# Output norm's deviation by ScalarE's root and a VectorE refinement in place of GpSimd's power, and three more blocks of spike additions on GpSimd

## What is computed

```python
def lif(x, v_th): return (x - v_th >= 0)            # a "spike", 0 or 1
def layer_norm(x, g, b):
    return (x - mean(x)) * rsqrt(var(x) + 1e-5) * g + b

# attention, 16 heads of 16
Q, K, V = (lif(layer_norm(xn @ W.T + bias, g, beta), 1.0) for each of q, k, v)
attn = 16 - (q_sum + k_sum.T - 2 * Q @ K.T) + log_pe_bias      # no softmax
out  = lif((attn * scale) @ V, 0.5)
out  = lif(layer_norm(out @ Wo.T + bo, go, betao), 1.0)

# experts: top 2 of softmax(xn @ router.T), scores made to sum to 1
h = xn @ up[e];  y = (silu(h[:256]) * h[256:]) @ down[e]
ffn = sum over the two experts of score * y

result = x + out + ffn
```

## Time and profile before

| | |
|---|---|
| median of 3 runs | 449.91 us (449.11 to 450.32) |
| the profiled execution, its own time | 448.21 us |
| its span in the profile | 446.3 us |
| mean granted clock of TensorE, share of full | 0.939 |
| TensorE busy | 389.5 us (87%) |
| VectorE busy | 283.8 us (64%) |
| ScalarE busy | 237.0 us (53%) |
| GpSimd busy | 210.7 us (47%) |

### The profile page before, as it was taken

The page is one execution under the profiler, slowest core; times in us unless marked ns, Lnnn a source line. Parts: engine busy times, 40 slices in busy tenths (PEclk is TensorE's granted clock), DMA queues, the critical chain, the costliest instruction groups (busy, mean ns, idle before and its releaser), DMA issues.

```text
span 446.3 us, 8933 instructions
## 1 busy us (share of the span) xinstructions
PE 389.5 (87%) x2585; PEld 318.6 (71%) x2586; DVE 283.8 (64%) x717; ACT 237.0 (53%) x756; POOL 210.7 (47%) x211
## 2 busy tenths in 40 slices
PE   4479956767999998899999999999999998999871
PEld 1223655767999997788888888888888875777550
DVE  5887899994777787644444444444444433479996
ACT  1436835342888888445445454454454543466650
POOL 3215330003677200177777777734333332369984
PEclk9596979686999999999999999999999999999976
DMA  8898150004533100444444444433222591992222
GB/s 278 245 343 295 46 208 1 0 1 149 166 99 106 47 0 20 138 143 150 144 149 154 144 148 146 138 120 107 94 94 94 183 336 48 383 379 75 95 95 95
DMA packets 44255, 63.12 MB, mean 141 GB/s; under 512 B 6022, under 2 KB 31622, under 8 KB 44232
## 3 DMA queue, kind: packets, MB, share of 16 engines
q1 hardware_dynamic: 35568, 42.65, 28.0%
q0 software_dynamic: 6816, 18.62, 13.0%
q10 hardware_dynamic: 1848, 1.58, 1.1%
HBM read 35.82 MB, written 17.70 MB: 120 GB/s over the span
## 4 chain that ended last, share of the span: by engine, by line
PE 55%; DVE 15%; issue 9%; POOL 9%; DMA 4%; ACT 3%; SPq 3%; POOLq 0%; DVEq 0%; ACTq 0%
PE bank L1132 15%; PE bank L1134 14%; PE bank L1133 14%; POOL xres L719 4%; POOL xres L712 3%; PE bank L1291 3%; SPq L323 3%; DMA ew_f<-experts 2%; PE bank L1275 2%; PE bank L1207 2%; DVE in_row L928 2%; DMA vec_d<-two_col 2%; DVE exT_l L959 2%; ACT gact L546 2%; POOL rstd L704 1%
## 5 line engine op out<-in xcount | busy, mean ns | idle before, releaser
L688 POOL DMA_INDIRECT slot_y<-ey,dest x71 | 70.1, 987 | 107.2 <-ACT ey L562 91.7
L682 POOL DMA_INDIRECT xn<-xn_d,token x71 | 69.5, 978 | 66.8 <-DVE dest L955 43.6
L1031 DVE TENSOR_TENSOR hid<-gact,bank 128x256 f32<-128x256 f32 x71 | 29.9, 421 | 77.2 <-ACT gact L546 77.2
L1132 PE MATMUL bank<-ew,exT_h 128*128 x142 | 62.3, 439 | 5.2 <-DVE exT_l L959 5.1
L546 ACT ACTIVATE gact<-bank 128x256 f32<-128x256 f32 x71 | 27.4, 386 | 63.0 <-PE bank L1134 63.0
L1132 PE MATMUL bank<-w_h,xT_h 128*128 128x256 f32 x192 | 57.4, 299 | 0.0
L1133 PE MATMUL bank<-w_l,xT_h 128*128 128x256 f32 x192 | 57.2, 298 | 0.0
L1134 PE MATMUL bank<-w_h,xT_l 128*128 128x256 f32 x192 | 57.1, 297 | 0.0
L1133 PE MATMUL bank<-ew,exT_h 128*128 x142 | 55.9, 394 | 0.0
L1134 PE MATMUL bank<-ew,exT_l 128*128 x142 | 55.9, 394 | 0.0
L501 ACT ACTIVATE junk<-bank 128x256 bf16<-128x256 f32 x96 | 35.8, 380 | 31.5 <-PE bank L1134 31.4
(11 more groups left out here) (187 smaller groups left out, 975.0 us busy)
## 6 DMA issues: line engine op xcount, KB each, us to landing
ex<-xn SPq DMA_DIRECT2D x71, 128.0 KB, 2.2
y_tok<-slot_y SPq DMA_DIRECT2D x8, 1024.0 KB, 13.8
xres<-x SPq DMA_DIRECT2D x16, 256.0 KB
out<-xres SPq DMA_DIRECT2D x16, 256.0 KB, 2.1
xn<-x SPq DMA_DIRECT2D x6, 512.0 KB, 11.2
xn_d<-xn SPq DMA_DIRECT2D x3, 1024.0 KB, 9.2
ew_f<-experts SPq DMA_DIRECT2D x1, 2560.0 KB, 9.9
ew_f<-experts SPq DMA_DIRECT2D x1, 2048.0 KB, 11.1
```

The source lines that it names most:

```text
L682: pool.indirect_dma_start(xn[:, j % RING, :], None, xn_d, bass.IndirectOffsetOnAxis(ap=token[:, j:j + 1], axis=0)).then_inc(gathered[j % 4 ...
L688: pool.indirect_dma_start(slot_y, bass.IndirectOffsetOnAxis(ap=dest[:, j:j + 1], axis=0), ey[:, j % 4, :], None).then_inc(y_out[j % 4], 16)
L1031: v.tensor_tensor(hid[:, m % 2, :], gact[:, m % 2, :], h_ps[m % 2][:, F:2 * F], ALU.mult).then_inc(s["hid_done"], 1)
L1132: mm(dst, a_h, b_h, start=first, stop=False)
```

## The change

The output norm's deviation is no longer GpSimd's power of the variance. ScalarE takes a root of the sum of squares behind its squares (`out_deviation`), and VectorE refines it by a Heron step in `out_variance`: a reciprocal, a scalar_tensor_tensor and a tensor_tensor, each waiting for the one before. The comparison in `spike_out` becomes `thr * std <= w`. GpSimd has no `out_rstd` any more. `LATE` is 14: GpSimd adds the spikes of blocks 11, 12 and 13 too. In both stages the factors are taken out of the step: the root is that of the sum (no 1/D), with D times eps as its bias, the step gives twice the root, and the threshold is multiplied by 0.5 / sqrt(D) once at the start; that spares the projection's `deviations` its first VectorE operation, `veps`.

```diff
-LATE = 11
+LATE = 14
@@ ScalarE
-                nc.scalar.activation(std[:, r, :], ssq[:, r, :], ACT.Sqrt, scale=1.0 / D, bias=eps_c[:, 0:1]).then_inc(s["std_done"], 1)
+                nc.scalar.activation(std[:, r, :], ssq[:, r, :], ACT.Sqrt, bias=eps_c[:, 0:1]).then_inc(s["std_done"], 1)
...
             def out_squares(a):
                 if a >= 2:
-                    act.wait_ge(s["w_var"], a - 1)
+                    act.wait_ge(s["w_var"], 3 * (a - 1))
...
+            def out_deviation(a):
+                act.wait_ge(s["w_ssq"], B * (a + 1))
+                nc.scalar.activation(std[:, a % 2, 0:B], ssq[:, a % 2, 0:B], ACT.Sqrt, bias=eps_c[:, 0:1]).then_inc(s["w_std"], 1)
...
                 if 1 <= a <= NB:
                     out_squares(a - 1)
+                    out_deviation(a - 1)
@@ GpSimd
-            g.memset(eps_c[:, :], EPS).then_inc(s["eps_set"], 1)
+            g.memset(eps_c[:, :], D * EPS).then_inc(s["eps_set"], 1)
...
-            def out_rstd(a):
-                pool.wait_ge(s["w_var"], a + 1)
-                if a >= 2:
-                    pool.wait_ge(s["w_spk"], B * (a - 1))
-                g.tensor_tensor(rstd[:, a % 2, 0:B], veps[:, a % 2, 0:B], neg_half[:, 0:B], ALU.pow).then_inc(s["w_rstd"], 1)
...
             for a in range(NB):
-                out_rstd(a)
                 if 1 <= a <= LATE:
                     add_spikes(a - 1)
@@ VectorE
-            v.tensor_tensor(two_col[:, 0, :], lim, far, ALU.add).then_inc(s["two_set"], 1)
+            v.scalar_tensor_tensor(two_col[:, 0, :], lim, 0.5 * D ** -0.5, far, ALU.mult, ALU.add).then_inc(s["two_set"], 1)
...
             def deviations(t, m, pair):
                 r = m // 2 % 2
-                dve.wait_ge(s["ssq_done"], G3 * (t + 2))
-                v.tensor_scalar(veps[:, r, :], ssq[:, r, :], 1.0 / D, EPS, ALU.mult, ALU.add).then_inc(s["heron"], 1)
                 dve.wait_ge(s["std_done"], pair + 1)
                 v.reciprocal(inv_std[:, r, :], std[:, r, :]).then_inc(s["heron"], 1)
-                v.scalar_tensor_tensor(inv_std[:, r, :], veps[:, r, :], 0.5, inv_std[:, r, :], ALU.mult, ALU.mult).then_inc(s["heron"], 1)
-                v.scalar_tensor_tensor(std[:, r, :], std[:, r, :], 0.5, inv_std[:, r, :], ALU.mult, ALU.add).then_inc(s["heron"], 1)
+                v.scalar_tensor_tensor(inv_std[:, r, :], ssq[:, r, :], D * EPS, inv_std[:, r, :], ALU.add, ALU.mult).then_inc(s["heron"], 1)
+                v.tensor_tensor(std[:, r, :], std[:, r, :], inv_std[:, r, :], ALU.add).then_inc(s["heron"], 1)
...
             def out_variance(a):
-                dve.wait_ge(s["w_ssq"], B * (a + 1))
-                v.tensor_scalar(veps[:, a % 2, 0:B], ssq[:, a % 2, 0:B], 1.0 / D, EPS, ALU.mult, ALU.add).then_inc(s["w_var"], 1)
+                dve.wait_ge(s["w_std"], a + 1)
+                r, n = a % 2, 3 * a
+                v.reciprocal(inv_std[:, r, 0:B], std[:, r, 0:B]).then_inc(s["w_var"], 1)
+                dve.wait_ge(s["w_var"], n + 1)
+                v.scalar_tensor_tensor(inv_std[:, r, 0:B], ssq[:, r, 0:B], D * EPS, inv_std[:, r, 0:B], ALU.add, ALU.mult).then_inc(s["w_var"], 1)
+                dve.wait_ge(s["w_var"], n + 2)
+                v.tensor_tensor(std[:, r, 0:B], std[:, r, 0:B], inv_std[:, r, 0:B], ALU.add).then_inc(s["w_var"], 1)

             def spike_out(a):
-                dve.wait_ge(s["w_rstd"], a + 1)
+                dve.wait_ge(s["w_var"], 3 * (a + 1))
                 for b in range(B):
-                    v.scalar_tensor_tensor(spk[:, a, b, :], w_ps[a % 2][:, b * D:(b + 1) * D], rstd[:, a % 2, b:b + 1],
-                                           thr_r[:, G3 * D:], ALU.mult, ALU.is_ge).then_inc(s["w_spk"], 1)
+                    v.scalar_tensor_tensor(spk[:, a, b, :], thr_r[:, G3 * D:], std[:, a % 2, b:b + 1],
+                                           w_ps[a % 2][:, b * D:(b + 1) * D], ALU.mult, ALU.is_le).then_inc(s["w_spk"], 1)
```

More of the change, by code:

```diff
@@ L261, in spiking_moe @@
             dve_order pool_order w_gone
-            s_done o_done o_turned oT_set out_proj w_ssq w_var w_rstd w_spk gated moe_added spk_added fin_done late_done out_done xres_in""".split()
+            s_done o_done o_turned oT_set out_proj w_ssq w_var w_std w_spk gated moe_added spk_added fin_done late_done out_done xres_in""".split()
         names.append("eps_set")
@@ L971, in deviations @@
                 r = m // 2 % 2
-                dve.wait_ge(s["ssq_done"], G3 * (t + 2))
-                v.tensor_scalar(veps[:, r, :], ssq[:, r, :], 1.0 / D, EPS, ALU.mult, ALU.add).then_inc(s["heron"], 1)
                 dve.wait_ge(s["std_done"], pair + 1)
                 v.reciprocal(inv_std[:, r, :], std[:, r, :]).then_inc(s["heron"], 1)
-                dve.wait_ge(s["heron"], pair * 4 + 2)
-                v.scalar_tensor_tensor(inv_std[:, r, :], veps[:, r, :], 0.5, inv_std[:, r, :], ALU.mult, ALU.mult).then_inc(s["heron"], 1)
-                dve.wait_ge(s["heron"], pair * 4 + 3)
-                v.scalar_tensor_tensor(std[:, r, :], std[:, r, :], 0.5, inv_std[:, r, :], ALU.mult, ALU.add).then_inc(s["heron"], 1)
-                dve.wait_ge(s["heron"], pair * 4 + 4)
+                dve.wait_ge(s["heron"], pair * 3 + 1)
+                v.scalar_tensor_tensor(inv_std[:, r, :], ssq[:, r, :], D * EPS, inv_std[:, r, :], ALU.add, ALU.mult).then_inc(s["heron"], 1)
+                dve.wait_ge(s["heron"], pair * 3 + 2)
+                v.tensor_tensor(std[:, r, :], std[:, r, :], inv_std[:, r, :], ALU.add).then_inc(s["heron"], 1)
+                dve.wait_ge(s["heron"], pair * 3 + 3)
             def spikes(t, m, half):
```

## The result

The changed kernel takes 457.36 us (median of 4 runs, 455.72 to 458.71), the kernel before 450.12 in the same comparison: a ratio of 1.0161, interval 1.0119 to 1.0204, that is 7.2 us slower. The forecast was 456.0, 5.9 us above that median of 450.12. The profiled execution took 455.72 around a span of 453.9.

The account below looks back on a forecast made before the run. It took VectorE's output-stage order, stalled behind GpSimd's adds, as the bound: start +0.9, three cycles of 14.05 us bringing block 15 to +8.1, tail -2.0, sum +6.1 on 449.91, so 456.0 us; range 450.9 to 459.8.

Parts of the forecast that it names:

- Its adds then run exactly when VectorE comes to operations with two SBUF inputs: Output stage: without the power, GpSimd starts its add of spikes once they are done, and VectorE's two-SBUF-input operations queue.
- a reciprocal that queues: Output refinement: the reciprocal also waits behind GpSimd's adds; 14.7 us per three blocks, 458.0 us in all; chance 0.12.
- small operations that don't: Output refinement: its small operations never wait behind GpSimd's adds; 12.5 us per three blocks, 450.9 us in all; chance 0.12.
- tensor_tensor 0.73, in the gap: Output refinement: the sum starts 0.73 us after the reciprocal, between two GpSimd adds, and is not blocked.
- some 14 of the 32 L1089s near 1.4 us: Sign in the output stage: about 14 of VectorE's 32 expert sums blocked, near 1.4 us instead of the median 0.476.
- over 12: Sign in the output stage: TensorE's wait for output spikes grows from 4.3 us to over 12.
- The start of the cycles: Output stage: block 6's reciprocal at 404.6, 0.9 us later than block 6's variance in the kernel before.
- The last cycle: Output blocks 12 to 15: 14.05 us like the others, missing output spikes (0.66 each) set against waits for last projections.
- The tail: From block 15's reciprocal to the last compute: 2.9 us instead of 4.9, so -2.0.
- the port's hold: How long a GpSimd add blocks VectorE: 1.04 or 1.10 us, entering about 12 waits, 1.2 us uncertainty in all.
- The moved adds: Spikes of blocks 11 to 13 added by GpSimd instead of VectorE: some 1.2 us of the 6.1 us rise.
- The faster rival: Output stage: GpSimd's adds end before the first expert sum asks, TensorE sets the pace; -6.5 us, 443.4; chance 0.10.

Follow-up runs that it names:

- the rows' edit: ScalarE's gated expert rows written to two PSUM banks, so expert sums read one SBUF tensor: 446.05 us in the kernel before, 452.49 in the changed kernel.

## Why the prediction was right, point by point

**The mechanism: shown.** "Its adds then run exactly when VectorE comes to operations with two SBUF inputs" is what the block above shows, and three edits tell it apart from the chain's latency and from the moved adds: two change where an operand stands (the second with a wait on ScalarE added), one only when GpSimd starts. The Trainium skill (SBUF — State Buffer, Who interferes with whom) says that a VectorE instruction with two SBUF inputs contends with a GpSimd one that reads SBUF, and that one with a single SBUF input, outside the two-port modes, does not; the trace agrees for these operations: 1.22 us for two elements from SBUF, 0.16 or 0.17 with one of the inputs in PSUM, and 0.17 at most for the reciprocal. That rule took the forecast's side against the rivals of a reciprocal that queues and of small operations that don't, and both are excluded.

One SBUF input alone is no safe conduct, though. The variance of the kernel before, a tensor_scalar with one, took up to 1.03 us beside an add; the prediction used it as evidence that small operations queue. What sets it apart from the reciprocal, which didn't, no run here tests.

**The step that was mis-sized: "tensor_tensor 0.73, in the gap".** In the working L1095 slipped through between two adds and the first expert sum was caught instead. In the trace L711 starts 0.51 before the reciprocal and not 0.55, and frees the port 1.11 after its own start and not 1.08, so L1093 ends 0.77 after the reciprocal's start and not 0.70, and L1095 asks at 410.59, 0.81 after it and not 0.73. L718 had started at 410.50 and had the port. So L1095 is caught (1.22), and the expert sums run free for one add. That moves the stall rather than doubling it, but each of the three kinds of block comes out longer: 4.19, 4.97 and 5.28 us (reciprocals at 404.50, 409.78, 413.97 and 418.94) for 4.08, 4.87 and 5.10. 14.44 a cycle instead of 14.05, three times, is 1.2 of the 1.55 us by which the last compute came later than forecast (7.65 for 6.1). My sign of "some 14 of the 32 L1089s near 1.4 us" was wrong for the same reason: six of them are over 1.4, as in the kernel before, and the stall shows at L1095 instead. TensorE's wait, at 11.8 us, stayed just under the "over 12" of the signs.

**The start of the cycles** (+0.9) came out as 404.50 against 403.69, +0.8; counted from the first output spike, which starts 0.2 earlier in this execution, it is +1.0, and the whole rise 7.8 (75.5 against 67.6). **The last cycle** was 14.86, 0.4 above the others. I had set the missing output spikes, twice 0.66, against waits for the last projections. That came out close by luck: VectorE hardly waits there at all, and it is more queueing that uses up the saving. In block 14 GpSimd's adds catch L1093, which takes 1.21 us instead of 0.59, and two of the four expert sums, which take 3.77 us together instead of the 1.66 of block 11. **The tail** was put at 2.9; 448.22 to 451.19 is 2.97. **The median**, 457.36, lies within the 454.5 to 457.6 given for this case alone, near its upper end; its rise of 7.2 compares with 6.1, and the two timings of the kernel before differ by 0.2. The working gives 1.2 of uncertainty for the port's hold; the bounds are 0.3 and 0.4 wider, and only the lower one has a term for that, the projection's 0.5.

**Costed at nothing, and nothing:** the projection stage and the table load (block 3's output spike ended at 385.19, and TensorE turned it at 385.91, behind its own products). The drain that the Trainium skill adds to a load (ScalarE: Activation LUTs, What ACT_TABLE_LOAD costs) does not show: 0.02 us lie between the load and the root. The roots on ScalarE brought the refinement 0.33 later, as forecast: counted from the first output spike, block 5's reciprocal starts at 23.96 us, where its variance started at 23.63.

**The moved adds** were given 1.2 us of the sum. Taking them back gave 2.3 with overlapping intervals, and the stage 2.1: the term was too small, if anything.

**The faster rival** at 443.4 had TensorE's pace and a shorter tail. Once the operands were moved its time was reached, 443.8, though not in its way: in the changed kernel, from block 5 on, GpSimd's adds were not over when VectorE asked. Part of the 5.4 us is no merit of the change, since the kernel before gains 2.7 from the rows' edit too. The rest is: ratio 0.9879 (0.9857 to 0.9901) against 0.9940 (0.9918 to 0.9963), some 2.7 us, though the one without the change still has the queue at its variance. The plan, less work for GpSimd, was sound once the port was out of the way.

## What to carry to other kernels

Count the operations of VectorE with two SBUF inputs beside GpSimd's adds before moving work from one to the other, and with them any one-input operation whose longest time in the profile is far above its shortest; a two-element operation can cost nearly as much as the whole add that it meets (1.22 us beside one of 1.30), and everything behind it in its engine's order pays. Where an operand could stand in PSUM, the queue was gone at no cost in operations. And an engine that is relieved starts its other work earlier: ask what that work will then collide with.

## What the runs showed of the hardware that I had not expected

Whether a small operation passes between two GpSimd adds that follow each other is decided within 0.2 us: L1095 asked 0.09 us after L718 had started and took over 1 us, in eight blocks of this execution. In block 13 it asked 0.10 us before L718 started and passed:

```profile
439.44 0.16 DVE L1095 TENSOR_TENSOR std<-std,inv_std 128x2 f32<-128x2 f32 x1
...
439.54 1.27 POOL L718 TENSOR_TENSOR xres<-xres,y_tok 128x512 f32<-128x512 f32 x1
```

In my working it asked 0.08 us earlier than it did, still 0.01 behind the start of L718. Whether it would have passed there, no run shows.

A wait that only delays GpSimd's adds made the changed kernel faster by 5 us (ratio 1.0049 for 1.0161), with the same work on every engine. And the kernel before, whose GpSimd looked full at 9.4 us of 10, gained 2.7 us from moving an operand of VectorE.
